# GNN and MoE megakernel on one core: prologue regrouped (2, 4, 4 tiles, six transpose banks, products between) and the adjacency set-up in eight steps

## The reference, cut to what matters

```python
def _layernorm(x, axis=-1, eps=1e-05):
    m = jnp.mean(x, axis=axis, keepdims=True)
    v = jnp.var(x, axis=axis, keepdims=True)
    return (x - m) / jnp.sqrt(v + eps)

def _L0_gnn_ref(X, W, edge_src, edge_dst, edge_vals):
    Z = jnp.matmul(X, W)
    msg = Z[edge_src] * edge_vals[:, None]
    agg = jax.ops.segment_sum(msg, edge_dst, num_segments=X.shape[0])
    return jax.nn.relu(agg)

x = x + _L0_gnn_ref(_layernorm(x, axis=-1), L0_gnn_W, src, dst, edge_weight)
x = x + _L0_ffn_ref(_layernorm(x, axis=-1)[None], ...)[0]      # attention and 64 experts
x = x + _L1_gnn_ref(_layernorm(x, axis=-1), edge_index, ...)   # mean of neighbours, batch norm
x = x + _L1_ffn_ref(_layernorm(x, axis=-1)[None], ...)[0]      # 8 experts
```

## Time and profile before

| | us |
|---|---|
| median of three runs | 1537.0 |
| lowest and highest | 1534.64, 1538.38 |
| the profiled execution, its own time | 1538.04 |
| its span in the trace | 1536.3 |
| TensorE busy | 1376.0 (90%) |
| VectorE busy | 737.4 (48%) |
| ScalarE busy | 471.4 (31%) |
| GpSimd busy | 226.3 (15%) |

### The profile page before, as it was taken

The page is one execution under the profiler, slowest core; times in us unless marked ns, Lnnn a source line. Parts: engine busy times, 40 slices in busy tenths (PEclk is TensorE's granted clock), DMA queues, the critical chain, the costliest instruction groups (busy, mean ns, idle before and its releaser), DMA issues. The chain is left out here.

```text
span 1536.3 us, 23873 instructions
## 1 busy us (share of the span) xinstructions
PE 1376.0 (90%) x7657; PEld 912.8 (59%) x7658; DVE 737.4 (48%) x1546; ACT 471.4 (31%) x1153; POOL 226.3 (15%) x355
## 2 busy tenths in 40 slices
PE   4799999989989999999776999999899998649969
PEld 2388874445457777777355666666545555536642
DVE  7299966562167777776453222222250012533421
ACT  4299960021045555554111111111340011201111
POOL 2033320000000000000111222222320000002224
PEclk9999999999999999999876999999899999659998
DMA  5000000020000000000524999999520000913326
GB/s 148 1 1 0 0 27 1 0 83 0 0 28 1 1 1 1 1 2 1 154 67 131 326 328 333 327 323 330 167 75 0 0 0 0 304 31 115 123 91 180
DMA packets 94017, 142.34 MB, mean 93 GB/s; under 512 B 13245, under 2 KB 50515, under 8 KB 93823
## 3 DMA queue, kind: packets, MB, share of 16 engines
q1 hardware_dynamic: 69267, 97.52, 20.5%
q0 software_dynamic: 14976, 26.81, 6.2%
q10 hardware_dynamic: 9708, 17.12, 3.3%
HBM read 115.09 MB, written 26.29 MB: 92 GB/s over the span
## 5 line engine op out<-in xcount | busy, mean ns | idle before, releaser
L1147 PEld LDWEIGHTS ps<-b_r 128*128 128x128 f32 x1024 | 127.6, 196 | 34.2 <-issue 32.6
L899 DVE TENSOR_REDUCE b_row_max<-ps 125x1 f32<-125x1251 f32 x80 | 116.5, 1456 | 62.0 <-PE ps L800 62.0
L1147 PE MATMUL ps<-b_r 128*128 128x78 f32 x1024 | 125.6, 277 | 1.1 <-DVE b_r L1208 1.1
L1156 PE MATMUL ps<-b_r 128*78 128x512 f32 x256 | 121.8, 599 | 0.0
L493 PE MATMUL ps<-b_r 125*125 125x160 f32 x660 | 119.4, 317 | 0.0
L465 ACT ACTIVATE b_r<-b_r 125x125 f32<-125x125 f32 x330 | 107.8, 389 | 15.0 <-DVE b_r L417 10.6
L1192 ACT ACTIVATE b_r<-ps,b_r 128x78 f32<-128x78 f32 x128 | 34.6, 322 | 228.5 <-PE ps L1147 228.5
L800 PE MATMUL ps<-b_r 64*125 64x417 f32 (+1 forms) x480 | 97.0, 534 | 7.1 <-ACT b_r L872 4.7
L834 PE MATMUL ps<-b_r 125*64 125x125 f32 x1600 | 94.7, 272 | 1.1 <-DVE b_r L859 1.1
L1051 POOL TENSOR_TENSOR b_x<-b_x,b_r 125x512 f32<-125x512 f32 x10 | 12.7, 1267 | 550.5 <-DVE b_r L997 550.5
L493 PEld LDWEIGHTS ps<-b_r 125*125 125x125 f32 x660 | 93.0, 189 | 1.2
(11 more groups left out here) (257 smaller groups left out, 2216.2 us busy)
## 6 DMA issues: line engine op xcount, KB each, us to landing
b_r<-L_ffn_w SPq DMA_DIRECT2D x128, 512.0 KB, 10.4
y<-b_r ACTq DMA_DIRECT2D x64, 156.0 KB
b_r<-L_ffn_W SPq DMA_DIRECT2D x2, 4096.0 KB, 20.2
y<-b_r ACTq DMA_DIRECT2D x24, 256.0 KB, 2.4
rows<-b_r SPq DMA_DIRECT2D x2, 2400.0 KB
out<-b_x SPq DMA_DIRECT2D x10, 240.0 KB
y<-b_r SPq DMA_DIRECT2D x1, 2048.0 KB, 11.3
b_x<-x SPq DMA_DIRECT2D x2, 960.0 KB
```

Of the source, the lines that this page charges most:

```text
L899: link(dve.tensor_reduce(T.row_max[:, slot:slot + 1], T.ps[:P, 3 * h:3 * h + 3, 0:CW], AX.XY, ALU.max))
L1147: last = pe.matmul(T.ps[:, 2 + r % 2, f * CAP:(f + 1) * CAP], T.ew1[r % WS][:, k, f * 128:(f + 1) * 128], T.ex_t[:, r % 2, k, :], start=(k ...
L1156: last = pe.matmul(T.ps[:CAP, 4 + r % 2, :], T.eh[:, r % 2, f, :], T.ew2[r % WS][:, f, :], start=(f == 0), stop=(f == FK - 1))
```

## The change

The prologue works in other groups (`FIRST_GROUPS`: tiles 0 and 1, 2 to 5, 6 to 9), for the loads of x, the turns and the copies. The turns go round six banks (2 to 7). TensorE's order becomes: turn of group 0, wait for W0, product 0, turn of group 1, products 1 to 3, turn of group 2, products 4 and 5, wait for all twelve copies (the edge lists go into the banks that the turns use), turn of the edge lists, products 6 to 9. ScalarE's order becomes: roots of tiles 0 to 3, copies of group 0, roots 4 to 6, product row 0, copies of group 1, roots 7 to 9, product rows 1 to 3, copies of group 2, product rows 4 to 9.

For the adjacency pass, the multiply-add of the high digit takes in the destination (one instruction with a tensor as second operand instead of one with a constant), the numbers of the cells begin at one, and the window start is kept less one; two of the ten steps thereby go. The two number rows are copied into PSUM at the end of the edge columns, in the prologue, instead of at the start of the adjacency block.

```diff
--- before.py
+++ after.py
@@ -31,6 +31,7 @@
 KD = D // 128
 EPS = 1e-5
 GROUPS = [(0, 4), (4, 4), (8, 2)]
+FIRST_GROUPS = [(0, 2), (2, 4), (6, 4)]
 CHUNKS = [(0, 417), (417, 417), (834, 416)]
@@ -102,10 +103,10 @@
 TURNS = len(GROUPS) * KD
-def transpose_group(pe, T, rows, ready, S, use, g, first=0, banks=8):
-
-
-    t0, n = GROUPS[g]
+def transpose_group(pe, T, rows, ready, S, use, g, first=0, banks=8, groups=GROUPS):
+
+
+    t0, n = groups[g]
     if ready is not None:
         pe.wait_ge(ready, t0 + n)
     for k in range(KD):
@@ -118,9 +119,9 @@
         last.then_inc(S.tiles_turned, 1)
-def copy_group(act, T, out, S, use, g, first=0, banks=8):
-
-    t0, n = GROUPS[g]
+def copy_group(act, T, out, S, use, g, first=0, banks=8, groups=GROUPS):
+
+    t0, n = groups[g]
     for k in range(KD):
         j = g * KD + k
         act.wait_ge(S.tiles_turned, use * TURNS + j + 1)
@@ -202,8 +203,9 @@
     dve.tensor_copy(T.base_all, T.ps[:P, 4, NCH:NCH + NG])
     link(dve.tensor_reduce(T.further[0:1, 0:1], T.ps[0:1, 5, NCH:NCH + NG], AX.X, ALU.max))
     link(dve.tensor_copy(T.passes[:], T.further[0:1, 0:1]))
-    link(dve.tensor_scalar(T.hi_col, T.hi_col, float(WD), 1.0, ALU.mult, ALU.add))
-    dve.sem_inc(S.columns_ready, 1)
+    link(dve.scalar_tensor_tensor(out=T.hi_col, in0=T.hi_col, scalar=float(WD), in1=T.dst_col, op0=ALU.mult, op1=ALU.add))
+    dve.tensor_copy(T.ps[:EC, 4, 0:P], T.lo_iota[:]).then_inc(S.iotas_copied, 1)
+    dve.tensor_copy(T.ps[:EC, 4, P:P + WC], T.cell_iota[:]).then_inc(S.iotas_copied, 1)
 def turn_edges(pe, T, S):
@@ -235,7 +237,7 @@
                                pattern=[[1, P]], channel_multiplier=-1)
             exact = dict(allow_small_or_imprecise_dtypes=True)
             pool.iota(T.row_iota[:], [[1, 128]], base=0, channel_multiplier=0, **exact)
-            pool.iota(T.cell_iota[:], [[1, WC]], base=0, channel_multiplier=0, **exact)
+            pool.iota(T.cell_iota[:], [[1, WC]], base=1, channel_multiplier=0, **exact)
             pool.iota(T.win_starts[:], [[WD, WINDOWS]], base=0, channel_multiplier=0, **exact).then_inc(S.starts_ready, 1)
             pool.iota(T.expert_iota[:], [[1, E0]], base=0, channel_multiplier=0, **exact)
             pool.iota(T.block_iota[:], [[1, NB]], base=0, channel_multiplier=0, **exact)
@@ -247,7 +249,7 @@
         @block.sync
         def _(sp):
             x_rows = A.x.rearrange("(t p) d -> p t d", t=NT)
-            for g, (t0, n) in enumerate(GROUPS):
+            for g, (t0, n) in enumerate(FIRST_GROUPS):
                 sp.dma_start(T.x[0:120, t0:t0 + n], x_rows[0:120, t0:t0 + n]).then_inc(S.x_loaded[g], 16)
             sp.dma_start(T.w_a, A.L0_gnn_W.rearrange("(k p) n -> p k n", k=KD)).then_inc(S.w0_loaded, 16)
             sp.dma_start(T.w_b, A.L0_ffn_wq.rearrange("(k p) n -> p k n", k=KD)).then_inc(S.wq_loaded, 16)
@@ -262,7 +264,7 @@
             dve.memset(T.ones[:], 1.0).then_inc(S.ones_ready, 1)
             dve.memset(at[:, BY_ACT:BY_ACT + BY_DVE], 0.0)
             for t in range(NT + 1):
-                for g, (t0, _) in enumerate(GROUPS):
+                for g, (t0, _) in enumerate(FIRST_GROUPS):
                     if t == t0:
                         dve.wait_ge(S.x_loaded[g], 32)
                 if t < NT:
@@ -285,25 +287,29 @@
             act.wait_ge(S.ones_ready, 1)
             act.activation(at[:, 0:BY_ACT], T.ones[:P, 0:1].to_broadcast([P, BY_ACT]), ACT.Copy, scale=0.0)
-            def product_rows(g):
-                for t in tiles_of(g):
+            def product_rows(tiles):
+                for t in tiles:
                     act.wait_ge(S.z_done, t + 1)
                     act.activation(T.rows_a[:, t, :], T.ps[:P, t % 2, :], ACT.Copy).then_inc(S.z_copied, 1)
-            row_roots(act, T, range(0, 6), S.z_var, S.z_std)
-            copy_group(act, T, T.feats, S, 0, 0, 2, 2)
-            row_roots(act, T, range(6, NT), S.z_var, S.z_std)
-            copy_group(act, T, T.feats, S, 0, 1, 2, 2)
-            product_rows(0)
-            copy_group(act, T, T.feats, S, 0, 2, 2, 2)
-            product_rows(1)
-            product_rows(2)
+            row_roots(act, T, range(0, 4), S.z_var, S.z_std)
+            copy_group(act, T, T.feats, S, 0, 0, 2, 6, FIRST_GROUPS)
+            row_roots(act, T, range(4, 7), S.z_var, S.z_std)
+            product_rows([0])
+            copy_group(act, T, T.feats, S, 0, 1, 2, 6, FIRST_GROUPS)
+            row_roots(act, T, range(7, NT), S.z_var, S.z_std)
+            product_rows(range(1, 4))
+            copy_group(act, T, T.feats, S, 0, 2, 2, 6, FIRST_GROUPS)
+            product_rows(range(4, NT))
         @block.tensor
         def _(pe):
-            def products(g):
+            def turn(g):
+                transpose_group(pe, T, T.rows_a, S.z_rows, S, 0, g, 2, 6, FIRST_GROUPS)
+
+            def products(g, tiles):
                 pe.wait_ge(S.tiles_copied, (g + 1) * KD)
-                for t in tiles_of(g):
+                for t in tiles:
                     if t >= 2:
                         pe.wait_ge(S.z_copied, t - 1)
                     for k in range(KD):
@@ -312,14 +318,17 @@
                     last.then_inc(S.z_done, 1)
             pe.wait_ge(S.ident_ready, 1)
-            transpose_group(pe, T, T.rows_a, S.z_rows, S, 0, 0, 2, 2)
-            transpose_group(pe, T, T.rows_a, S.z_rows, S, 0, 1, 2, 2)
+            turn(0)
             pe.wait_ge(S.w0_loaded, 16)
-            products(0)
-            transpose_group(pe, T, T.rows_a, S.z_rows, S, 0, 2, 2, 2)
-            products(1)
+            products(0, [0])
+            turn(1)
+            products(0, [1])
+            products(1, [2, 3])
+            turn(2)
+            products(1, [4, 5])
+            pe.wait_ge(S.tiles_copied, TURNS)
             turn_edges(pe, T, S)
-            products(2)
+            products(2, range(6, NT))
 def adjacency(nc, T, S, A):
@@ -382,17 +391,15 @@
                 dve.wait_ge(S.at_added, r * NG + 2)
                 dve.wait_ge(S.ct_added, r * NG + 2)
                 steps = [
+                    lambda: dve.tensor_scalar(T.base_now, T.base_all, float(LAST_WINDOW), 1.0, ALU.min, ALU.subtract),
                     lambda: dve.tensor_tensor(T.rel_col, T.dst_col, every, ALU.subtract),
-                    lambda: dve.tensor_scalar(T.base_now, T.base_all, float(LAST_WINDOW), None, ALU.min),
-                    lambda: dve.tensor_copy(T.base_row[:], T.base_now[0:1, :]),
+                    lambda: dve.tensor_scalar(T.base_row[:], T.base_now[0:1, :], 1.0, None, ALU.add),
+                    lambda: dve.tensor_tensor(T.cell_col, T.hi_col, T.base_now.unsqueeze(2).to_broadcast([EC, NG, CJ]),
+                                              ALU.subtract),
                     lambda: dve.tensor_scalar(T.valid_col, T.rel_col, 0.0, None, ALU.is_ge),
                     lambda: dve.scalar_tensor_tensor(out=T.valid_col, in0=T.rel_col, scalar=float(WD), in1=T.valid_col,
                                                      op0=ALU.is_lt, op1=ALU.mult),
-                    lambda: dve.tensor_tensor(T.cell_col, T.dst_col, T.base_now.unsqueeze(2).to_broadcast([EC, NG, CJ]),
-                                              ALU.subtract),
-                    lambda: dve.tensor_tensor(T.cell_col, T.cell_col, T.hi_col, ALU.add),
                     lambda: dve.tensor_tensor(T.cell_col, T.cell_col, T.valid_col, ALU.mult),
-                    lambda: dve.tensor_scalar(T.cell_col, T.cell_col, 1.0, None, ALU.subtract),
                     lambda: dve.tensor_scalar(T.base_all, T.base_all, float(WD), None, ALU.add),
                 ]
                 for i, step in enumerate(steps):
@@ -429,8 +436,6 @@
                     dve.wait_ge(S.counts_done, seen + (i + 1))
                     add_counts(sums, seen, i - 2)
-            dve.tensor_copy(lo_iota, T.lo_iota[:]).then_inc(S.iotas_copied, 1)
-            dve.tensor_copy(cell_iota, T.cell_iota[:]).then_inc(S.iotas_copied, 1)
             dve.wait_ge(S.iotas_copied, 2)
             dve.sem_inc(S.ct_added, 2)
             visits(dve, "dve", body, next_pass, last_counts)
```

## The result

| | before | after |
|---|---|---|
| median, seven runs each, us | 1539.03 | 1531.55 |
| lowest and highest, us | 1534.64, 1547.93 | 1528.34, 1533.51 |
| ratio after to before, 95% interval | | 0.9935 (0.9907 to 0.9963) |
| profiled execution: its time, its span, us | 1538.04, 1536.3 | 1529.28, 1527.6 |
| VectorE's first comparison of the adjacency loop, us | 74.09 | 68.94 |

The kernel became faster, by 0.65% with 0.37 to 0.93% as the interval. The predicted 1532.3 us lies 0.75 us from the measured median, but the kernel before came out at 1539.0 over seven runs instead of 1537.0 over three, so that the gain, 7.5 us by the medians and 10 us by the ratio, is larger than the 4.7 us of the forecast. Weighted by their intervals, the three give 0.9957, or 6.6 us, with 4.7 to 8.5 us as the interval.

The account below looks back on a forecast made before the run. TensorE was taken to set the prologue's end, VectorE the set-up's. TensorE's end 3.3 us earlier (6.5 - 1.7 - 1.45 - 0.05), plus 0.5 and 0.9, made 4.7 us off 1537.0: 1532.3 us, range 1529.5 to 1535.2.

Parts of the forecast that it names:

- Part 1, W0: Prologue: products start when W0's load lands at 22.27 us, so at 22.5 instead of 28.96 us, 6.5 us earlier.
- Part 2, the turns: Prologue: turns of sixteen transposes take 1.7 us without bank waits; the turn of tiles 2 to 5 adds 1.7 us.
- Part 3, the clock: First products after TensorE's idle wait run at the low clock level for 4.5 us; 1.45 us lost against today.
- Rival (a): The clock is already up at the first products, as printed; the 2.25 us loss goes, 1530.0 us; chance 0.10.
- (b): Prologue: the slow stretch outlasts tile 0 and the next turn; loss 4 instead of 2.25 us, 1534.0 us; chance 0.20.
- (d): Slower: the clock stays low through the mixed products and turns; low until 45.5 us gives 1541.6 us; chance 0.08.
- The slacks: Prologue: VectorE and ScalarE work comes later, but 5.4 us remain before the last turn and 5.6 before the edge turn.
- Part 4, the set-up: Adjacency set-up: moving the number-row copies frees 0.5 us, and eight steps instead of ten save 0.9 us.
- rival (c): The set-up does not start earlier after the copies; only fewer steps count, 1532.8 to 1533.5 us; chance 0.10.

Follow-up runs that it names:

- w0_early: The changed kernel with W0's load queued ahead of the third x group, and products 0 and 1 both ahead of the second turn; ratio to before 0.9939.
- two_banks: The changed kernel with the turns going round two PSUM banks instead of six, groups and order kept; one run, 1534.21 us.
- prologue_only: The changed kernel with the old set-up: ten steps, cell numbers from zero, number rows copied in the adjacency block; ratio to before 0.9986.
- pad4: The changed kernel with four tiny one-column memsets added on VectorE at the end of its prologue part, ahead of the adjacency loop; one run, 1531.92 us.
- pe_warm: The changed kernel with unread identity transposes on TensorE, 90 ahead of the first turn and 50 before the wait for W0; ratio to before 0.9932.
- setup_only: The kernel before with only the new set-up: eight steps, cell numbers from one, number rows copied in the prologue; ratio to before 0.9985.

## Why the prediction was right and where it failed

**The lean towards no change failed, and behind it one sentence.** I had the gain at 4.7 us, the line of what can be told from no change at 4.6, and gave no change 0.49 against 0.47. The step that failed is the first paragraph's: that all later stages run the same instructions and so move as a block, by which everything behind the loop's start was put at nothing. The adjacency loop runs the same instructions, but with five recorded instructions fewer ahead of it on VectorE, and was 0.85 us shorter over its length (141.98 to 141.13 us). With it and the 5.15 us of the loop's start the sum is 6.0 us, on the far side of the line and near the pooled 6.6. What the first set of runs shows beyond that, up to 10 us, did not come again; that its median stands 0.75 us from the forecast's 1532.3 is luck in part, as the gain was larger and the kernel before stood 2 us higher than the three runs said.

**Where the 8.7 us between the first two traces are:** 5.15 at the loop's start, 0.85 in the loop, 0.8 between loop and first experts (these sum to the 6.8 at the experts), and 1.9 behind, where the traces of one kernel differ by as much (708.6 to 711.0 us before, 706.7 to 709.3 after). The 0.8 us were there in two of three pairs and not in the third; I leave their cause open as a whole. They are a balance of stages that come out longer and shorter, and in one of these the reason can be read (TensorE's order of time and windows as above, before and after):

```profile
317.23 35.51 PE L697 MATMUL ps<-b_r,b_w_b 128*128 128x417 f32 x96 [0.72 <-PEq L615]
...
320.00:321.00 1.00, 1.00 (x3) 0.53 (x2) 1.00 (x1) 0.00 (x0) 0.00 (x0) 0.68 0.98 362
```

```profile
311.22 36.43 PE L702 MATMUL ps<-b_r,b_w_b 128*128 128x417 f32 x96 [0.72 <-PEq L620]
...
316.00:317.00 1.00, 1.00 (x3) 0.52 (x2) 1.00 (x1) 0.10 (x1) 0.00 (x0) 0.76 1.03 383
```

The same 96 matmuls take 0.92 us more after the change: the granted clock rose within the microsecond from 320 us before, some 3.4 us into them, and within that from 316 after, some 5.3 us into them; half of the difference is the 0.9 us. So a stage that nobody touched loses or gains by how long TensorE stays low at its restart.

**Part 1, W0:** right. It landed 19.7 us after its issue, and the product started at 22.07 instead of the 22.5 of the forecast: 0.2 us are the landing (22.03 for 22.27), 0.2 a weight load too many in the sum. w0_early shows that it is the bound.

**Part 2, the turns:** right, 1.71 us each for 1.7, no bank waits; two_banks prices what the six banks save, 1.2 us.

**Part 3, the clock:** right in kind and, by luck, in size: a low stretch of about 4.3 us for 4.5, product 0 in 5.64 us for 5.7. But the size is not fixed: 5.16 us in prologue_only, 6.61 in pad4, for the same instructions. My ends of 1.45 and 2.45 us for the loss were too narrow on one side: 6.61 - 3.43 = 3.2 us. Rival (a), the printed 1.00, is refuted by pe_warm: with TensorE busy before, the product takes 3.53 us, under the same print. The rule of the Trainium skill (TensorE: Matmul & The Clock Gate, Part 1: The HAM clock gate) that the low level is the default and activity releases it agrees with this. Rivals (b) and (d), a low level that lasts on through turns and products, came in no trace of the changed kernel.

**The slacks:** right in place, with more room: rows 6 to 9 at 33.6 us (forecast 34.8), the edge preparation at 41.84 (43.2), needed at 48.30.

**Part 4, the set-up:** right, 1.42 us to the first step and 3.19 us of steps; rival (c) is refuted by setup_only, which has both numbers with the old prologue. The clock fell before the loop as forecast, and rose at 74 us.

## What to carry to other kernels

A matmul stage that is pulled ahead to the end of a load comes behind an idle wait, and in these traces its first microseconds ran at the low level; count that loss, or keep TensorE busy with unread work while it waits (here 2.1 us in a product, and 1.5 us in the first ten groups of a loop). Where the expected gain stands at the line of what can be measured, small things that no diff shows (the place of a loop in an engine's instruction stream, the low stretch at a restart far behind the change) decide on which side it comes out; the forecast should then not call either side the likelier.

## What the runs showed of the hardware that I had not expected

The same loop on VectorE costs 0.11 us more per iteration when four instructions are put ahead of it (12.89 against 13.00 us; 13.02 in the kernel before, with five more), as a hole in VectorE's own queue at the turn of the iteration. The granted clock prints 1.00 at the start of the traces while the durations are those of the low level (weight loads 0.33 us, against 0.19 in pe_warm at the same print). A transfer of 1 MB with 0.98 MB less queued ahead of it on the same queue landed only 2.9 us earlier. Up to the first experts at 827 us, three traces of the kernel before agreed within 0.3 us, and most of the scatter of its whole executions came after that; of the changed kernel's three traces one was over 2 us late there already.
